# Node products of a graph network: a seven-trip loop written out, its transposes one chunk ahead, its tables stored chunk by chunk

## The reference

```python
# layer 0
h = x @ W_w + W_b
# layer 1
h = concatenate([x[row], edge_attr]) ; h = relu(h @ W1a + b1a) @ W1b + b1b
z = concatenate([x, agg, u[batch]]) ; return relu(z @ W2a + b2a) @ W2b + b2b
# layer 2, twice (128 -> 256, then 256 -> 128), and a skip at its end
xl = (x @ Wl + bl) ; xr = (x @ Wr + br) ; m = xl[src] + xr[dst] + ee
return h + (x @ skipW + skipb)
# layer 3, three times
m = concatenate([x[dst], x[src] - x[dst]]) ; h = relu(m @ W1 + b1) @ W2 + b2 ; segment_max(h, dst)
```

## Time and profile before

| | |
|---|---|
| median of 3 runs | 11837.31 us (11834.0 to 11841.89) |
| the profiled execution, its own time | 11841.19 us |
| its span in the profile | 11839.4 us |
| mean granted clock of PE | 0.742 of full speed |
| PE busy | 7849.9 us (66%) |
| DVE busy | 7062.0 us (60%) |
| POOL busy | 6678.2 us (56%) |
| ACT busy | 2661.2 us (22%) |
| HBM read and written | 1115.44 MB and 320.07 MB |

### The profile page before, as it was taken

One profiled execution on the slowest core, in us unless ns is written; L12 is line 12 of the kernel. 1 busy time (PEld: TensorE's weight loads), 2 busy tenths in 40 slices (PEclk: granted clock), 3 DMA queues, 4 the chain that ended last, 5 costly groups with the idle time before them and its releaser, 6 DMA issues. The chain is left out here.

```text
span 11839.4 us, 182004 instructions
## 1 busy us (share of the span) xinstructions
PE 7849.9 (66%) x39163; PEld 6599.3 (56%) x39164; DVE 7062.0 (60%) x13587; ACT 2661.2 (22%) x8800; POOL 6678.2 (56%) x6703
## 2 busy tenths in 40 slices
PE   4995444437886377764654777563788778877886
PEld 3995444426775355542433666462566556655665
DVE  4445454444444289995675666566566656665666
ACT  1331000001111200004651000131333333333333
POOL 0006888846775077762322777330677667766776
PEclk6555666655555799997986666675899889988998
DMA  3114555543221167764532444330444344434444
GB/s 108 38 39 85 95 96 97 95 91 84 81 81 55 24 224 244 245 217 102 157 115 61 153 152 153 105 111 27 138 154 154 124 138 154 150 128 138 154 150 137
DMA packets 828292, 1435.96 MB, mean 121 GB/s; under 512 B 182864, under 2 KB 494268, under 8 KB 787760
## 3 DMA queue, kind: packets, MB, share of 16 engines
q1 hardware_dynamic: 531136, 981.94, 25.7%
q0 software_dynamic: 297072, 453.23, 17.0%
HBM read 1115.44 MB, written 320.07 MB: 121 GB/s over the span
## 5 line engine op out<-in xcount | busy, mean ns | idle before, releaser
L1614 POOL DMA_INDIRECT T<-gather_d,srci x2508 | 2459.3, 981 | 1263.4 <-issue 755.6
L827 POOL DMA_INDIRECT added_d<-T,slots x832 | 1296.3, 1558 | 281.5 <-issue 219.7
L1198 PE MATMUL PS<-T,ident 128*128 128x256 f32 (+1 forms) x3328 | 1069.2, 411 | 453.8 <-DMA T<-wide_d,srci 244.7
L1147 POOL DMA_INDIRECT T<-wide_d,srci x832 | 860.4, 1034 | 673.5 <-PEq L71 420.1
L1147 POOL DMA_INDIRECT T<-gather_d,srci x832 | 820.1, 986 | 531.7 <-PEq L71 278.3
L1196 PE MATMUL PS<-T 128*128 x3328 | 1004.3, 392 | 139.9 <-issue 98.5
L1418 PE MATMUL PS<-T 128*128 128x260 f32 (+1 forms) x3328 | 806.7, 403 | 424.0 <-DVEq L1471 349.6
L1198 PEld LDWEIGHTS PS<-T,ident 128*128 128x128 f32 x3328 | 672.4, 236 | 705.7 <-DMA T<-wide_d,srci 347.6
L940 POOL DMA_INDIRECT T<-gather_d,srci x832 | 792.8, 953 | 439.1 <-issue 253.7
L1397 POOL TENSOR_TENSOR T<-T,LG 128x256 f32<-128x256 f32 (+1 forms) x840 | 429.6, 532 | 998.6 <-PE PS L1418 753.7
L1418 PEld LDWEIGHTS PS<-T 128*128 128x128 f32 x3328 | 634.5, 240 | 596.2 <-DVEq L1471 329.8
(11 more groups left out here) (252 smaller groups left out, 16011.4 us busy)
## 6 DMA issues: line engine op xcount, KB each, us to landing
T<-quads_d SPq DMA_DIRECT2D x315, 1024.0 KB
T<-edge_rows_d SPq DMA_DIRECT2D x210, 512.0 KB
edge_rows_d<-T SPq DMA_DIRECT2D x209, 512.0 KB, 2.8
T<-onehot_t_d SPq DMA_DIRECT2D x416, 256.0 KB
T<-gather_d,srci POOLq DMA_INDIRECT x4172, 2.6
T<-edge_rows_d SPq DMA_DIRECT2D x210, 256.0 KB
onehot_t_d<-T SPq DMA_DIRECT2D x208, 256.0 KB, 3.4
edge_rows_d<-T SPq DMA_DIRECT2D x208, 256.0 KB, 2.1
```

Of the source, the lines that this page charges most:

```text
L827: gp.indirect_dma_start(added_d[u][:, :], bass.IndirectOffsetOnAxis(ap=slots[:, k:k + 1], axis=0), part(OUT[r], u), None, compute_op=ALU.a ...
L1147: gp.indirect_dma_start(part(R[n % RING], u, width), None, table[:, :], bass.IndirectOffsetOnAxis(ap=srci[:, k:k + 1], axis=0)).then_inc(r ...
L1198: last = T_.matmul(spot(i, u), ident[:, :], part(R[r], u, width), start=False, stop=True)
L1614: gp.indirect_dma_start(part(R[n % RING], u), None, gather_d[:, :], bass.IndirectOffsetOnAxis(ap=srci[:, k:k + 1], axis=0)).then_inc(rows_ ...
```

## The change

`node_linear` becomes straight code for its seven chunks on each engine.

- PE reads the blocks of the source where they lie: the first copy by ACT (L446) is gone.
- PE does the transposes of chunk j + 1 before the products of chunk j. Transposed groups alternate between two parts of PSUM (`turn`), ACT's copies of them between two sets in `stage` (`room(j, k)`), outputs between two other parts of PSUM (`sums`).
- An output may carry `store`: SP then starts a transfer of each chunk of that table as soon as DVE has written it, and at the end waits for all seven.
- `table_to_dram` is gone, and so are its six blocks. The two stages L1552 and L1554 become one with four outputs (K1 n4), the stored one second, with LG as scratch. L1571 writes its second output straight into T2, so ACT's copy L1578 and its block are gone. In layer 3 the stored output comes first.

There are 11 stages after.

```diff
-            room = [stage[:, k * NB * DIM:(k + 1) * NB * DIM] for k in range(2 * K)]
+            room = lambda j, k: stage[:, (j % 2 * K + k) * NB * DIM:(j % 2 * K + k + 1) * NB * DIM]
+            turn = lambda q: PS[:, 1024 * (q % 2):1024 * (q % 2) + NB * DIM]
+            sums = lambda o: PS[:, 2048 + 1024 * (o % 2):2048 + 1024 * (o % 2) + NB * DIM]
...
+                @block.tensor
+                def _(pe):
+                    def transposes(j):
+                        for k in range(K):
+                            q = j * K + k
+                            if q >= 2:
+                                pe.wait_ge(turned_out.h, turned_out.at(q - 1))
+                            for u in range(NB):
+                                last = T_.transpose(part(turn(q), u), cut(srcs[k], j)[:, u], ident[:, :])
+                            last.then_inc(turned.h, 1)
+
+                    def products(j):
+                        pe.wait_ge(turned_out.h, turned_out.at((j + 1) * K))
+                        for n, o in enumerate(outs):
+                            if j * n_out + n >= 2:
+                                pe.wait_ge(added.h, added.at(j * n_out + n - 1))
...
+                    transposes(0)
+                    for j in range(chunks):
+                        if j + 1 < chunks:
+                            transposes(j + 1)
+                        products(j)
...
-                    with act.Fori(0, BLOCKS // NB) as j:
-                        act.wait_ge(pB[0].h, pB[0].at(j * n_out + 1))
+                    for j in range(chunks):
                         for k in range(K):
-                            S_.activation(room[k].rearrange("p (u w) -> p u w", w=DIM), view(srcs[k], j),
-                                          ACT.Copy).then_inc(aA[0].h, 1)
-                        for k in range(K):
-                            act.wait_ge(pA[0].h, pA[0].at(j * K + k + 1))
-                            S_.activation(room[K + k], PS[:, 1024 * (k % 2):1024 * (k % 2) + NB * DIM], ACT.Copy).then_inc(aB[0].h, 1)
...
+                            act.wait_ge(turned.h, turned.at(j * K + k + 1))
+                            if j >= 2:
+                                act.wait_ge(products_made.h, products_made.at((j - 1) * n_out))
+                            S_.activation(room(j, k), turn(j * K + k), ACT.Copy).then_inc(turned_out.h, 1)
...
+                @block.sync
+                def _(sp):
+                    for j in range(chunks):
+                        for n in stores:
+                            sp.wait_ge(added.h, added.at(j * n_out + n + 1))
+                            sp.dma_start(outs[n]["store"][j * NB * P:(j + 1) * NB * P, :].rearrange("(t p) f -> p t f", p=P),
+                                         view(outs[n]["to"], j)).then_inc(stored.h, 16)
+                    if stores:
+                        sp.wait_ge(stored.h, stored.at(16 * chunks * len(stores)))
...
-            node_linear([(H, DIM, 0)], [dict(w=[wcol(k)], add=wcol(4 + k), to=(T1, WIDE, k * DIM)) for k in range(2)], T2)
-            table_to_dram(T1, WIDE, wide_d)
-            node_linear([(H, DIM, 0)], [dict(w=[wcol(2 + k)], add=wcol(6 + k), to=(T2, WIDE, k * DIM)) for k in range(2)], T1)
+            node_linear([(H, DIM, 0)], [dict(w=[wcol(0)], add=wcol(4), to=(T1, WIDE, 0)),
+                                        dict(w=[wcol(1)], add=wcol(5), to=(T1, WIDE, DIM), store=wide_d),
+                                        dict(w=[wcol(2)], add=wcol(6), to=(T2, WIDE, 0)),
+                                        dict(w=[wcol(3)], add=wcol(7), to=(T2, WIDE, DIM))], LG)
...
-            table_to_dram(T1, DIM, gather_d)
-            with nc.Block() as block:
-                @block.scalar
-                def _(act):
-                    S_.activation(T2[:, 0:ROWS], T1[:, ROWS:2 * ROWS], ACT.Copy)
...
-                table_to_dram(T1[:, ROWS:2 * ROWS], DIM, gather_d)
+                node_linear([(H, DIM, 0)], [dict(w=[wcol(1)], add=wcol(5), to=(T1[:, ROWS:2 * ROWS], DIM, 0), store=gather_d),
+                                            dict(w=[wcol(0)], add=wcol(3), to=(T1, DIM, 0))], T2)
```

More of the change, by code:

```diff
@@ new lines, in node_linear @@
+            cut = lambda spec, j: view(spec, j)[:, :, spec[2]:spec[2] + DIM]
+            room = lambda j, k: stage[:, (j % 2 * K + k) * NB * DIM:(j % 2 * K + k + 1) * NB * DIM]
+            turn = lambda q: PS[:, 1024 * (q % 2):1024 * (q % 2) + NB * DIM]
+            sums = lambda o: PS[:, 2048 + 1024 * (o % 2):2048 + 1024 * (o % 2) + NB * DIM]
+            stores = [n for n, o in enumerate(outs) if o.get("store") is not None]
+            with nc.Block() as block:
+                @block.tensor
[13 more added lines that the diff above has]
+                                pe.wait_ge(added.h, added.at(j * n_out + n - 1))
+                            for u in range(NB):
+                                for k in range(K):
+                                    last = T_.matmul(part(sums(j * n_out + n), u), part(room(j, k), u), o["w"][k],
+                                                     start=k == 0, stop=k == K - 1)
+                            last.then_inc(products_made.h, 1)
+                    transposes(0)
[3 more added lines that the diff above has]
+                        products(j)
@@ L452, in _ @@
[L452 to L473, removed]
@@ L477, in _ @@
                     c = vch.on(dve)
-                    dve.sem_inc(v2_done.h, 2)
-                    with dve.Fori(0, BLOCKS // NB) as j:
-                        c.open(j, sum((o.get("plus") is not None) + bool(o.get("relu")) for o in outs))
+                    for j in range(chunks):
                         for n, o in enumerate(outs):
[L482 to L485, removed]
+                            dve.wait_ge(products_made.h, products_made.at(j * n_out + n + 1))
+                            src, to = split(sums(j * n_out + n)), cut(o["to"], j)
                             if o.get("plus") is not None:
-                                c.link(V.tensor_tensor(to, src, view(o["plus"], j), ALU.add))
+                                c.link(V.tensor_tensor(to, src, cut(o["plus"], j), ALU.add))
                                 src = to
@@ L492, in _ @@
                                 last = V.tensor_scalar(to, to, 0.0, None, ALU.max)
[L493 to L497, removed]
+                            last.then_inc(added.h, 1)
+                @block.sync
+                def _(sp):
+                    for j in range(chunks):
+                        for n in stores:
[4 more added lines that the diff above has]
+                        sp.wait_ge(stored.h, stored.at(16 * chunks * len(stores)))
+            for s, n in ((added, chunks * n_out), (products_made, chunks * n_out), (turned, chunks * K),
+                         (turned_out, chunks * K), (stored, 16 * chunks * len(stores))):
                 s.passed(n)
@@ L856, in add_messages @@
             vv_done.passed(COPIES)
-        def table_to_dram(tab, width, dst):
-            with nc.Block() as block:
[L860 to L864, removed]
         def layer0():
@@ L1571, in layer2 @@
             node_linear([(T2, WIDE, 0), (T2, WIDE, DIM)],
[L1572 to L1578 removed]
+                        [dict(w=[wcol(0), wcol(1)], add=wcol(4), to=(T1, DIM, 0), store=gather_d),
+                         dict(w=[wcol(2), wcol(3)], add=wcol(5), to=(T2, DIM, 0))], LG)
             load_weights([(0, P, bias_row(flat(I["L2_att2"]))), (DIM, P, bias_row(flat(I["L2_We2"])))])
```

14 lines of the change are left out of this document (4 added, 10 removed).

## The result

The changed kernel takes **11459.1 us** (median of 4 runs, 11453.6 to 11464.7) beside 11835.7 for the kernel before in the same comparison (4 runs, 11830.4 to 11841.9). The ratio is 0.9682 with an interval of 0.9665 to 0.9698. The profiled execution took 11464.7 us, against 11841.2 before.

A forecast was written before the change was run, and what follows sets the result against it. Serial chains between barriers were taken to bound the kernel. Stages 261.2 us less plus store gaps 81.1 less make 342.3; from the profiled 11841.2 that gives 11499, and 11495 for the median, range 11460 to 11575.

The forecast's parts named there:

- what bounds a stage: Node stages: serial chain of ACT copies and PE work with almost no overlap; 625.0 us would become 363.8, 261.2 less.
- The predicted slip of 0.5 us: Stages with `plus`: DVE's two additions, some 2.3 us a chunk against PE's 2.42, just fit; 0.5 us added for slips.
- the stores: Gaps behind six stages that store a table: 93.5 us would become 12.4, 81.1 less, only the last chunk showing.
- code costs nothing: PE's written-out node stages: about 4600 more instructions, 19 more packets, cost taken as 0, with 49 us kept for the range.
- The mark of 1090 us: Edge maxima: taking longer than 1090 us in the changed profile was listed as a sign that the prediction was wrong.
- the cold start of 3.4 us a stage: Every node stage starts at the low clock, half speed for 6.8 us, losing 3.4; range term -15 to +10 us.
- seven more transposes at 0.85 us: PE's work in a node stage: a further seven transposes at the high clock cost about 0.85 us, from 1.82 and 0.98.
- their sum: The eleven node stages, added stage by stage, were forecast at 363.8 us against 625.0 before.
- 20 us either way: Range term for the unchanged edge loops, whose clock might be granted a little differently: some 20 us either way.
- The small stages did not stay cold: Rival: K1 n1 stages stay at the low clock, 61 us for five, 11556, chance 0.09; all eleven cold, 11735, 0.02.
- Stores and code did not show: Rival: the seven-part stores or PE's code fetches show in the stages, 67 us, giving 11562; chance 0.09.
- the slower case: Rival: edge loops refetch code, 156 branch returns in the edge maxima at 2.6 us, 406 us more, 11901; chance 0.03.

The follow-up runs named there:

- stores apart: Changed kernel with each stored table written by one transfer in a block of its own behind its stage, as before the change; 11532.5 us, ratio 0.9732.
- its repeat: The changed kernel run once more, nothing altered, in a later set of runs with a second trace; 12764.4 us, ratio 0.9692 to the kernel before.
- a later comparison: Later set of runs: kernel before and changed kernel repeated, plus two with 17 or 26 identity transposes while weights load; kernel before 13171.0 us, changed 12764.4.

## Why the prediction was right and wrong

**Right: what bounds a stage, and what happens to it.** The chain of the earlier trace rows opened as worked out. After a stage's start PE waits for next to nothing; of all product groups one waited for ACT, 0.2 us. ACT makes 91 copies. The predicted slip of 0.5 us in the stages with `plus` did not come: DVE's 2.2 us a chunk just fit into 2.33.

**Right: the stores, to 1 us.** Predicted 12.4 for the six gaps, measured 11.7. L1058 has 4.07 for 3.9, the merged stage 1.33 for 1.3, L1571 0.27 for 0.3, layer 3 has 2.00 for 2.3. The bound from rows of 512 and 256 KB was good for a chunk of 448. The experiment with stores apart gives 76 us for this part alone; the rest of the 81.9 is ACT's copy of 5.43 and the block end that went with it.

**Right: code costs nothing.** 31 packets came for about 32 predicted, with 0.4 us of pauses on PE inside the stages. The mark of 1090 us set for the edge maxima was passed, by 1 us, and means no refetch: one packet in each of the 52 trips would be 135 us, and the packets would be more than 31. The mark was too tight: the third edge maxima of the kernel before had itself taken 1090.3.

**Wrong: the cold start of 3.4 us a stage.** The step that failed is the start at the low clock, the term of 3.4 us in each stage's sum, which rests on a clock that rises "6.8 us after the first transposes". That number was read rightly (the trace has 6.80), but where PE pauses twice in a chunk, and it was carried into a stage without pauses. With the pauses gone the clock rose 3.2 to 5.9 us after the first transpose, 4.6 in the mean of ten stages, and one stage (3778.94) began at the high clock, 0.32 us after the end of the stage before it. Ten times 2.3 is 23 us, where eleven times 3.4 is 37: 14 us. The experiments show that it is the pauses. Three traces have no pauses inside a stage (the changed kernel, its repeat, stores apart): in their 30 stages that began at the low clock the rise came after 2.7 to 5.9 us. Five have one or two pauses a chunk: in their 45 one-source stages that began at the low clock it never came before 5.8 us, mostly after 6 to 9, and in six of them only after 12 to 50. The two-source stages, whose first transposes are twice as many, went either way with pauses (3.0 to 9.4). One pause or two made no difference to the first rise in most stages, but with two the clock fell again in many of them. The range had allowed 15 us for this term; it was used up.

**Wrong in size: seven more transposes at 0.85 us.** They cost 0.765. The chunk of 2.33 less 1.57 for the products leaves 0.76. The 0.85 was the difference of two rows of different stages, 1.82 and 0.98. In the earlier trace rows each row contains the delay of a group that starts after a pause; that these did not cancel is a likely reason, and it was not tested. 91 groups times 0.085 is 7.7 us. The range held nothing for this term.

Together with the slips these make 22.7 of the 23.1 us by which the stages beat their sum.

**The other 10 us** were not in the stages. By block: edge logits 6.6 less, weighted sums 3.4 less, add messages 1.3 less, the edge MLP 1.1 less, the setup 0.8 less, edge maxima 4.6 more, segment weights 1.1 more, and the first work of each of the eleven stages comes some 0.25 us sooner after the block ahead. The unchanged loops move this much between kernels. The first weighted sums of layer 2 took 712.5 us before, 713.8 after, 701.9 in the kernel with the loop written out and 695.6 with stores apart, and the granted clock goes with it (0.91, 0.91, 0.93 and 0.98):

```profile
5225.91:5939.74 713.83, 467.08 (x1664) 336.23 (x1664) 478.04 (x1043) 464.59 (x1890) 264.27 (x420) 0.91 0.51 154
```
```profile
5261.77:5957.41 695.64, 423.10 (x1664) 301.37 (x1664) 473.09 (x1043) 467.96 (x1890) 250.28 (x420) 0.98 0.53 158
```

(The first window is the changed kernel's, the second that of the stores apart.) The same 1664 matmuls, at 0.91 and at 0.98. Why it differs from kernel to kernel is open; no kernel here varied that loop. The range had 20 us either way for this, and 10 were needed, on the same side as the other two misses. That is how three small errors, all toward a faster kernel, left a range whose long side pointed the other way.

**The rivals.** The small stages did not stay cold (all at 0.87 or more), and no stage of the changed kernel fell back to the low clock once it had risen. In the repeat and with stores apart one did, L1099, briefly near its start. Stores and code did not show. Of the slower case nothing appeared.

## What to carry to other kernels

A pause between PE's groups costs twice: its own length, and, through the clock, part of the work around it. Taking 75 us of waits off PE's chain gave 138 us, 50 of them through the clock. When a change removes the pauses, no start-up time measured with them holds; take it from the densest stretch the trace has, as a lower end at least. A difference of some 10 us outside of what was changed is not yet a cost or a gain of the change. A hardware loop cost 0.17 us a chunk here, 15 us in the kernel, which no row of busy time showed. And a store that waits for a whole table costs its whole length, where one that follows chunk by chunk costs its last chunk: put the stored output first, and other work covers part or all of even that (gaps of 4.07, 2.00 and 0.27 us).

## What was not expected of the hardware

- The clock's first rise is later with pauses: 2.7 to 5.9 us after first work without them, 5.8 to 11.9 in one-source stages with one pause of 1.0 a chunk, and with two pauses of 1.1 it may come only at the end of the stage (51.2 us at 0.52). The Trainium skill ("TensorE: Matmul & The Clock Gate", "A second HAM failure mode: psum-queue depth-cycling") names small pauses as a cause of swings; these runs agree, and add that two stages with the same instructions and the same pauses went either way (0.52 and 0.81 in one kernel), as did one stage in two executions of the kernel before (0.65 and 0.90).
- Transposes alone bring the clock up: behind 17 of them, 3.80 us, stage L1058 began at the high clock.
- Eighteen more packets of PE's code (31 for 13) cost no time that shows, while the hardware loop that they replace cost 0.17 us a trip (6.59 and 6.42 us a chunk).
- The same kernel took 11% longer in a later comparison (13171.0 and 11855.7 us), nearly all of it in the loops that gather, with the same ratio between the two kernels (0.9692 and 0.9682). The cause is open.
